# A graph layer's third stage with its bias in the mixing matrix, its first steps among the last products of the stage before, and edges that start late

## The reference

```python
xn = layernorm(x)
def sage(x, Wl, Wr, b):                 # edges src -> dst
    agg = segment_sum(x[src], dst) / max(degree(dst), 1)
    return agg @ Wl.T + x @ Wr.T + b
h   = tanh(sage(xn, W1_l, W1_r, b1))
gnn = sage(h, W2_l, W2_r, b2)
q, k, v = split(xn @ w_qkv)             # 8 heads of 64
qp, kp = elu(q @ proj) + 1, elu(k @ proj) + 1
kv = sum over nodes of kp^T v           # per head, 64 x 64
z  = 1 / (qp @ sum over nodes of kp)    # per node and head
mix = (qp @ kv * z) @ w_proj + b_proj
x  = x + gnn + mix
out = x + top-1 mixture of 8 small experts(layernorm(x))
```

## Time and profile before

| | |
|---|---|
| median of three executions | 2788.45 us (2784.39 to 2789.29) |
| the profiled execution | 2787.47 us |
| its span, first to last instruction | 2785.7 us |
| busy: PE, DVE, POOL, ACT | 94%, 61%, 41%, 35% |
| granted TensorE clock, mean | 0.975 of full |
| HBM traffic | 502 MB in DMA packets, mean 180 GB/s |

### The profile page before, as it was taken

How to read it: one execution, slowest core, us unless ns; L and a number is a source line. 1 busy time by engine, 2 the same in 40 slices (tenths; PEclk the granted TensorE clock), 3 DMA queues, 4 the chain that set the end, 5 groups by cost and what they waited for, 6 DMA issues and landing times.

```text
span 2785.7 us, 36335 instructions
## 1 busy us (share of the span) xinstructions
PE 2614.7 (94%) x11712; PEld 2080.2 (75%) x11712; DVE 1698.5 (61%) x3626; ACT 987.7 (35%) x1725; POOL 1150.9 (41%) x1089
## 2 busy tenths in 40 slices
PE   4899999999999989999998699999999699999999
PEld 3688888888888868888886366666667477777777
DVE  2677777777777744444443455555554477777774
ACT  2455554444444434444443222222221123223232
POOL 3577776666666630000000666666666111111110
PEclk7899999999999999999999899999999799999999
DMA  9566666455555555655665688888887323233231
GB/s 377 174 185 184 188 172 167 125 154 128 151 128 141 137 165 202 237 221 220 225 226 200 208 249 272 236 241 266 245 242 203 128 91 133 94 109 117 90 136 46
DMA packets 140309, 502.45 MB, mean 180 GB/s; under 512 B 27288, under 2 KB 27800, under 8 KB 99776
## 3 DMA queue, kind: packets, MB, share of 16 engines
q1 hardware_dynamic: 104384, 417.15, 40.2%
q0 software_dynamic: 35840, 84.23, 16.7%
HBM read 261.60 MB, written 239.73 MB: 180 GB/s over the span
## 4 chain that ended last, share of the span: by engine, by line
PE 70%; POOL 10%; issue 9%; DMA 4%; DVE 4%; ACT 1%; SPq 1%; POOLq 0%; ACTq 0%; DVEq 0%
PE bank L1158 55%; PE bank L1209 8%; POOL agg_d L360 3%; PE bank L1165 3%; POOL m_x L688 2%; DMA agg_d<-O,eidx 2%; POOL G_low L313 2%; POOL G L345 2%; DVE x2T_low L313 2%; PE bank L1345 2%; DMA agg_d<-O 1%; SPq L467 1%; PE bank L401 1%; PE bank L402 1%; ACT f_relu L847 1%
## 5 line engine op out<-in xcount | busy, mean ns | idle before, releaser
L313 POOL TENSOR_TENSOR G_low<-G,G_high 128x512 fp32r<-128x512 f32 x160 | 211.2, 1320 | 342.9 <-ACT G_high L423 342.9
L360 POOL DMA_INDIRECT agg_d<-O,eidx x160 | 273.2, 1707 | 70.1 <-issue 37.6
L345 POOL DMA_INDIRECT G<-y_d,esrc x80 | 83.3, 1041 | 494.4 <-DMA erow<-in_dst 481.9
L1005 DVE TENSOR_TENSOR m_x<-bank,m_x 128x512 f32<-128x512 f32 x80 | 55.3, 692 | 289.6 <-POOL m_x L688 263.3
L705 POOL TENSOR_SCALAR veps<-mv 128x1 f32<-128x1 f32 x80 | 26.9, 336 | 494.9 <-DVE mv L1050 494.9
L826 ACT CAST qz_high<-low 128x512 fp32r<-128x512 f32 x80 | 49.7, 621 | 395.1 <-DVE low L1018 263.7
L381 DVE SCALAR_TENSOR_TENSOR Sj<-erow,dstf,tri 128x128 f32<-128x128 int32 x160 | 162.3, 1014 | 35.5 <-DMA agg_d<-O 28.7
L390 DVE SCALAR_TENSOR_TENSOR eidx<-cnt,todump,dstf 128x1 int32<-128x1 f32 x160 | 176.6, 1104 | 8.0
L423 ACT CAST G_high<-G 128x512 fp32r<-128x512 f32 x160 | 98.9, 618 | 215.5 <-DVE G L921 196.7
L1158 PE MATMUL bank<-xnT_high,Wq_high 128*128 128x512 f32 x320 | 125.6, 393 | 28.4 <-DVE xnT_low L313 28.4
L661 POOL TENSOR_TENSOR bias<-bias,low 128x512 f32<-128x512 f32 (+1 forms) x80 | 143.5, 1794 | 0.0
(11 more groups left out here) (196 smaller groups left out, 7807.6 us busy)
## 6 DMA issues: line engine op xcount, KB each, us to landing
agg_d<-O SPq DMA_DIRECT2D x20, 1040.0 KB, 19.4
b_agg<-agg_d SPq DMA_DIRECT2D x20, 1040.0 KB, 8.4
a_x<-in_x SPq DMA_DIRECT2D x20, 1024.0 KB, 6.8
agg_d<-z_halves SPq DMA_DIRECT2D x20, 1024.0 KB, 5.7
q_d<-q_rows SPq DMA_DIRECT2D x80, 256.0 KB, 2.4
r_d<-r_rows SPq DMA_DIRECT2D x80, 256.0 KB, 3.7
r_in<-r_d SPq DMA_DIRECT2D x20, 1024.0 KB, 4.8
hT_high_d<-hT_made_high SPq DMA_DIRECT2D x20, 1024.0 KB, 10.3
```

Source lines behind the costliest of these rows:

```text
L313: return eng.tensor_tensor(out_, full, high.bitcast(F32), ALU.subtract)
L345: pool.indirect_dma_start(G[:, j, :], None, table, bass.IndirectOffsetOnAxis(ap=esrc[:, b, j:j + 1], axis=0)).then_inc(e_g[j], 16)
L360: pool.indirect_dma_start(agg, bass.IndirectOffsetOnAxis(ap=eidx[:, j, 0:1], axis=0), O[:, j, 0:width], None, compute_op=ALU.add).then_inc ...
```

## The change

- **Bias.** The key features of head 0, multiplied by `z`, sum to one when weighted with the key sums, so adding (b2 + b_proj) times the key sums of head 0 to the first 128 rows of `M` adds the bias to every row of the result. DVE does it once (`m0`), from a bias loaded at the very start with two more constants' DMAs; the 80 additions on POOL and their semaphore go.
- **Hand-over.** PE's last four y products are written out by hand, with the denominators of groups 0 and 1 and the spreads of tiles 0 to 3 between them; ACT's copies of y alternate with its steps 0 to 4. SP loads `phi_q1`, the halves of h of groups 0 and 1 and the edge lists ahead of the last y store. `hT_low` moves from slot 12 to 16 of the arena, and other buffers with it.
- **Edges.** The table `mix_edges` gives the edge steps of each step of the stage: none for t < 8, one at 8 and 9, then one and two in turn up to t = 31 (35 in all), and from t = 32 one, three ahead of the tile. The second edge of a step stands after the product on PE. POOL's order is now low half, gather, scatter.
- **DVE's order** in a step: multiply by `phi_q`, edge build, add product, low half, reciprocal, `z` low half.
- **Zeros.** `agg1_d` is cleared from `zero`, in the place of `spare`; DVE no longer waits for it, POOL does ahead of the first scatter (step 7), and ACT ahead of the first use of `spare` (step 9, the splits start three steps later).
- **End of stage three.** SP loads the first edge sums `f_xn` of group 0 after product 76, that of group 1 after the last product and ahead of the expert weights.

```diff
@@ consts
-        split_at = (0, 6, 12, 18, 24, 30)
+        split_at = (0, 9, 15, 21, 27, 33)
+                  (bias[:], b2.to_broadcast([P, D])), (low[:, 1, :], bproj.to_broadcast([P, D]))]
+        mix_edges, done = [], 0
+        for t in range(32):
+            now = 0 if t < EDGE_FROM else 1 + (t % 2 if EDGE_EXTRA <= t < 32 else 0)
+            mix_edges.append([(s // 8, s % 8) for s in range(done, done + now)])
+            done += now
+        ahead = done - 32
+        def edge_steps(turn, k):
+            t = 8 * turn + k
+            if isinstance(t, int) and t < 32:
+                return mix_edges[t]
+            return [lagged(turn, k, -ahead)] if active(t, -ahead, NT + 5) else []
@@ edge_scatter (POOL), edge_build (DVE)
+                if ph == 0 and isinstance(i, int) and i == 0:
+                    pool.wait_ge(s_z1, 16 * NG)
-            if ph == 0 and isinstance(i, int) and i == 0:
-                dve.wait_ge(s_z1, 16 * NG)
@@ SP, start and end of stage two
-                sp.dma_start(agg1_g[g], O[:, :, :].rearrange("p j w -> p (j w)")).then_inc(s_z1, 16)
+                sp.dma_start(agg1_g[g], zero[:, :]).then_inc(s_z1, 16)
+                    if end:
+                        sp.dma_start(flat(phq[1]), q_d[1]).then_inc(m_ph[1], 16)
...
+                    if end:
+                        sp.wait_ge(b_hst, 64)
+                        for i in range(2):
+                            for n in range(2):
+                                sp.dma_start(flat(mhT[n], i), hT_d[n][i]).then_inc(m_ht[i], 16)
+                        for i in range(2):
+                            edge_load(sp, 1, 0, i)
                     sp.wait_ge(b_yo, 4 * g)
                     sp.dma_start(y_g[g - 1], flat(by, 1 - b)).then_inc(b_yst[1 - b], 16)
@@ SP, end of stage three
+            sp.wait_ge(m_p, NT - TG)
+            sp.wait_ge(e_sc, 16 * 2 * NT)
+            sp.dma_start(flat(fa[0]), agg2_g[0]).then_inc(f_a[0], 16)
             sp.wait_ge(m_qz, NT)
             sp.dma_start(flat(fx[0]), part_d[0]).then_inc(f_p[0], 16)
@@ POOL, mix
-                edge_scatter(pool, 1, turn, k, agg2_d.ap(), D)
-                edge_low(pool, 1, turn, k)
-                edge_gather(pool, 1, turn, k, y_d.ap())
-                if active(t, 8, NT):
...
-                    pool.tensor_tensor(xr, xr, bias[:, :], ALU.add).then_inc(m_xb, 1)
+                for te in edge_steps(turn, k):
+                    edge_low(pool, 1, *te)
+                    edge_gather(pool, 1, *te, y_d.ap())
+                    edge_scatter(pool, 1, *te, agg2_d.ap(), D)
@@ DVE, fold
+            dve.scalar_tensor_tensor(m0, bias[:, :], KS[:, 0, 0:1], bank[0][:, :], ALU.mult, ALU.add
+                                     ).then_inc(c_mb, 1)
@@ DVE, mix
-                    dve.wait_ge(m_xb, t - 8)
@@ PE, hand-over
+            pe.wait_ge(b_hs, NT - 1)
+            denominators(0, 0)
+            pe.wait_ge(b_hl, NT - 1)
+            y_product(NG, 0)
+            denominators(0, 1)
+            y_product(NG, 1)
+            spread(0, 2)
+            spread(0, 3)
+            y_product(NG, 2)
+            spread(0, 4)
+            spread(0, 5)
+            y_product(NG, 3)
```

197 lines of the change are left out of this document (112 added, 85 removed).

## The result

The changed kernel takes 2808.72 us in the median of four runs (2805.63 to 2813.87), beside 2788.87 for the kernel before on the same chip: 1.0076 times its time, 95% interval 1.0057 to 1.0096. It is slower by 20 us; I had predicted it faster by 80.

| stretch | before | after | difference |
|---|---|---|---|
| to ACT's last h tile (`hT_made_high`) | 1508.0 | 1486.7 | -21.3 |
| from there to the last addition to `m_x` | 666.5 | 722.1 | +55.6 |
| from there to DVE's first `f_x` of stage four | 53.7 | 39.0 | -14.7 |
| the rest | 557.6 | 560.9 | +3.3 |

The account below looks back on a forecast made before the run. PE's matmuls set most of the pace; stalls and a DVE-ACT-POOL ring over the bias were removable. Start -25, hand-over and stage three -42, stage end -12.6 sum to -79.6, giving 2708 us, own range 2690 to 2726.

Parts of the forecast that it names:

- the rivals' share: Whole time: the range widened to 2678 to 2745 us to take in rival forecasts of other times.
- The start: Start of the program: DVE's 28.7 us stall for clears goes, less costs coming back, -25 us in all.
- The hand-over: Between y products and stage three: first mixing product 38 us earlier, at about 1506 with the start's gain.
- The scatter interval in steps 11 to 31: Stage three, steps with 1.5 edges: POOL's serial scatters set the pace, 6.07 us each, 6.3 with long landings.
- the ring: Stage three before: DVE waits for POOL's bias addition, ACT for DVE, POOL for ACT; 30.7 us a group.
- My bound of 7.5: Stage three: upper bound of the scatter interval in us, from landings of 6.7 each; 34 us more in all.
- After step 32 PE binds at 28.3 to 28.6: Late stage three: PE's own need sets a group of four tiles at 28.3 to 28.6 us.
- Rival 2: Stage three after step 32: another ring holds 30.7 us a group, +29 us, 2737 us; chance 0.12.
- End of the stage: End of stage three: `f_xn` and `f_x` are there when the last product ends, -12.6 us.
- Rival 4: Stage three, steps 11 to 31: full DMA engines make every landing 9.2 us, +107 us, 2815 us; chance 0.04.
- The fold of the bias: Stage three: removing POOL's bias addition opens the only ring; its one added DVE instruction of 0.7 us is hidden.

## Why the prediction was wrong

The prediction gives 2690 to 2726 as its own range and 2678 to 2745 with the rivals' share; 2808.7 is outside both, and on the other side of before.

- **The start** (-25): -21.3. DVE's stall is gone; POOL waits 10.7 us for the clears (7 predicted) and PE 4.6 and 1.2 where I had 3 for both.
- **The hand-over** (first product at 1506): 1512.0, of which 3.7 us are the start's. PE's wait for `phi_q` of the third group, 6 us by the prediction, is 5.3 us. What I had not counted is the clock: with PE idle 2.1 us at 1509.6 and 5.3 at 1525 for want of input, the granted clock is 0.68 of full from 1510 to 1520 us and 0.72 from 1520 to 1532 (between the levels of 1.2 and 2.4 GHz), the first product takes 7.6 us instead of 5.45, and the denominators behind `phi_q` take 6.1 instead of 3.75. First scatter at 1553.7 instead of 1541: the step was right and mis-sized, +13.
- **The scatter interval in steps 11 to 31** (6.07, 6.3 with the long ones): 7.7 over the first 30 scatters. This is the step that failed. I took the landings from the kernel before, "since the median and the pattern of a group are the nearest rows", which made 5.3 us in the mean. But that pattern was made by the ring that the change removes: it kept a scatter 2.2 us behind the landing before it in the mean, h's loads 5 us ahead of a scatter, and the store 0.8 us behind its start. Out of the ring a scatter starts 0.84 us behind a landing in the mean, the loads fall where they fall, and landings are 7.1 in the mean. With the 13 us this puts step 32 at 1782.5 instead of 1727. My bound of 7.5 was also too low.
- **After step 32 PE binds at 28.3 to 28.6** (stage end 2107): 31.9 and 2208.8. Rival 2 had 30.7 by some other ring for +29; it was the scatter chain itself, which I had let bind only in the doubled steps, and it was longer than before's ring: +46.
- **End of the stage** (-12.6): -14.7. **Stage four** (0): +3.3.
- Together: 55.5 to step 32, 46 behind it, -2.1 and 3.3 make 102.7, which is the whole difference between -79.6 and +23.0 but for rounding.
- **Rival 4** (every landing 9.2, 2815, chance 0.04) is nearest in time and in kind: slower landings. Its reason, DMA engines filled by the 1.5 rate, was wrong. From 1850 to 2081 us the DMA share is 0.83 in both kernels, and the landings stay long at one edge a step. It should have had a chain that is always in flight as its condition, for which two rows spoke: the scatters of 9.2 and 6.7 us in the earlier trace rows both stood 5 us behind h's loads. And a mean landing of 8.3 was not needed to eat the gain: 7.1 did, since it held for the whole stage.
- The fold of the bias I had as the thing that frees the stage. By itself it costs 27 us; it pays only with the phase held.

## What to carry to other kernels

When a ring of waits is removed, the durations of what stood in it are not to be taken over: list what the ring kept apart (here a serial chain of indirect scatters and another queue's bulk loads), and price the step with them together. Here the serial DMA chain beside bulk loads needed both a hold on the chain and loads issued right behind each link; test the dose first by displacing one load. Before cutting a wait of 147 us, ask what is released earlier by it and whom that meets.
